# Latent attention: probabilities turned in 32x32 blocks by VectorE, values summed by eight tiles in four shared banks

## The reference

```python
q = (x @ W_q).reshape(B, S, 16, 128).transpose(0, 2, 1, 3)
latent = x @ W_kv_down                      # 64 wide
kv = (latent @ W_kv_up).reshape(B, S, 16, 128).transpose(0, 2, 1, 3)
scores = einsum('bhqd,bhkd->bhqk', q, kv) / sqrt(128)
probs = softmax(scores)
out = einsum('bhqk,bhkd->bhqd', probs, kv)
return out.transpose(0, 2, 1, 3).reshape(B, S, 2048) @ W_o
```

## Time and profile before

| | us |
|---|---|
| median of 3 runs | 1814.08 |
| lowest and highest | 1811.03 and 1816.03 |
| span of the profiled execution | 1840.4 |
| latent attention in it, first scores to last addition | 1195.4 to 1706.7 |

### The profile page before, as it was taken

One profiled execution on the slowest core, in us unless ns is written; L12 is line 12 of the kernel. 1 busy time (PEld: TensorE's weight loads), 2 busy tenths in 40 slices (PEclk: granted clock), 3 DMA queues, 4 the chain that ended last, 5 costly groups with the idle time before them and its releaser, 6 DMA issues. The chain is left out here.

```text
span 1840.4 us, 26235 instructions
## 1 busy us (share of the span) xinstructions
PE 1555.0 (84%) x7678; PEld 1023.0 (56%) x7678; DVE 1079.0 (59%) x2735; ACT 761.4 (41%) x1818; POOL 690.8 (38%) x677
## 2 busy tenths in 40 slices
PE   6889995548898978889993788689999999998798
PEld 3556654324455554555662566455666666665576
DVE  6842222376676547832224788477776766664788
ACT  5523332245555525533332111166655556553211
POOL 4553334454200003543335554055555545453000
PEclk9999997578999998999996888899999999999899
DMA  8319985122100005249972222000000000000000
GB/s 244 90 59 290 292 244 176 57 69 60 38 1 1 1 8 162 69 125 268 286 213 82 71 75 60 1 1 1 1 1 1 1 1 1 1 1 1 9 17 21
DMA packets 83395, 142.55 MB, mean 77 GB/s; under 512 B 15816, under 2 KB 43312, under 8 KB 83296
## 3 DMA queue, kind: packets, MB, share of 16 engines
q1 hardware_dynamic: 53600, 90.96, 17.0%
q0 software_dynamic: 15360, 37.77, 7.0%
q10 hardware_dynamic: 14336, 12.59, 2.5%
HBM read 122.39 MB, written 18.87 MB: 77 GB/s over the span
## 5 line engine op out<-in xcount | busy, mean ns | idle before, releaser
L2267 POOL TENSOR_TENSOR sb_m_prob<-sb_m_prob,sb_m_rinv 128x512 f32<-128x512 f32 x256 | 258.8, 1043 | 287.4 <-DVE sb_m_rinv L2316 287.4
L2223 ACT ACTIVATE sb_m_prob<-m_ps_s,sb_m_nmax 128x512 f32<-128x512 f32 x256 | 173.8, 683 | 204.1 <-DVE sb_m_nmax L2320 203.9
L1263 POOL DMA_INDIRECT sb_c_rows<-slot_rows,sb_slot x192 | 191.6, 998 | 130.7 <-DVEq L1284 57.9
L2320 DVE TENSOR_REDUCE sb_m_nmax<-m_ps_s 128x2 f32<-128x1024 f32 x128 | 156.4, 1222 | 127.8 <-PE m_ps_s L2118 127.8
L1097 POOL DMA_INDIRECT e_xn<-xn_rows,sb_table x128 | 118.0, 922 | 208.7 <-PE e_ps_x L1175 195.3
L1246 DVE TENSOR_TENSOR sb_e_h<-sb_e_sg,e_ps_gu 96x176 f32<-96x176 f32 x128 | 42.6, 333 | 255.2 <-ACT sb_e_sg L1222 208.7
L1184 PE MATMUL e_ps_gu<-e_wgu,sb_e_xT 128*96 128x352 f32 x512 | 177.2, 468 | 16.1 <-ACT sb_e_xT L1216 14.2
L2126 PE MATMUL m_ps_p<-sb_ident,sb_m_prob 128*128 128x128 f32 x1024 | 136.4, 273 | 15.8 <-ACT sb_m_pT L2231 11.3
L2126 PEld LDWEIGHTS m_ps_p<-sb_ident,sb_m_prob 128*128 128x128 f32 x1024 | 117.9, 141 | 41.2 <-POOL sb_m_prob L2267 13.8
L1201 PE MATMUL e_ps_y<-e_wdn,sb_e_hT 96*96 96x256 f32 x512 | 132.2, 382 | 0.0
L2117 PE MATMUL m_ps_s<-sb_m_latT_high,sb_m_qa 128*128 128x512 f32 x256 | 126.6, 495 | 1.1 <-ACT sb_m_prob L2223 1.1
(11 more groups left out here) (283 smaller groups left out, 3230.1 us busy)
## 6 DMA issues: line engine op xcount, KB each, us to landing
e_wgu<-wgu SPq DMA_DIRECT2D x128, 352.0 KB
e_wdn<-wdn SPq DMA_DIRECT2D x128, 192.0 KB
slot_rows<-sb_e_y ACTq DMA_DIRECT2D x128, 96.0 KB
xn_rows<-e_xn SPq DMA_DIRECT2D x16, 256.0 KB, 2.3
sb_c_rows<-slot_rows,sb_slot POOLq DMA_INDIRECT x192
sb_x<-x SPq DMA_DIRECT2D x4, 512.0 KB, 5.9
e_xn<-xn_rows,sb_table POOLq DMA_INDIRECT x128
sb_g_zm<-wqT SPq DMA_DIRECT2D x1, 2048.0 KB
```

Source lines behind the costliest of these rows:

```text
L1263: pool.indirect_dma_start(rows[u][j][:, :], None, k.slot_rows[:, :], bass.IndirectOffsetOnAxis(ap=k.slot[:, n, j:j + 1], axis=0))\
L2223: act.activation(prob[s % 4][:, hh, :], ps_s[s % 2][:, hh, :], ACT.Exp, bias=nmax[s % 2][:, hh:hh + 1], accum_out=rsum[s % 2][:, hh:hh + 1 ...
L2267: pool.tensor_tensor(part, part, rinv[s % 2][:, hh:hh + 1].to_broadcast([P, T]), ALU.mult)\
L2320: dve.tensor_reduce(nmax[s % 2][:, :], ps_s[s % 2][:, :, :], AX, ALU.max, negate=True).then_inc(nmax_ready, 1)
```

## The change

Only `latent_attention` changes; expert layers and linear attention stay as they are.

- The transposes on PE and both copies of them go. DVE turns each 32x32 block of `prob` in place of them, straight from SBUF to `pT`, one instruction a step (`probs_turned`), two steps behind. Blocks stay in their group of 32 partitions: partition group a then holds the probabilities of its own 32 queries of each tile, for 32 keys at a time, all 16 blocks of keys side by side.
- `values` becomes, for each of 16 blocks of 32 keys (kb), four partition groups (a) and two heads, a product of 32 rows x 64 columns x 128 columns of probabilities: 128 a pair. Group a sums into bank a of a `ps_v` that is now four banks. Half of a pair is made in each of two steps with s % 4 = 3 and 0.
- The latent must lie in each group of partitions with all keys: 16 DMAs a batch on SP's queue copy it from `lat` to `lat_rows`.
- The miscellany loses its own bank. It uses banks 0 and 1 of `ps_v` in turn, at steps with s % 4 = 1 and 2, and each of the two parts waits for the other: values for the eviction of the last two uses, the miscellany for the copy of the values.
- `oT_copy` goes from DVE to ACT, ahead of the exponentials of a step with s % 4 = 1.
- DVE's order becomes, for each s: row_max(s), probs_turned(s-2), inverse(s), and in steps with miscellany evictions(d) and preparations(d) of the same step. ACT's is oT_copy, exps(s), miscellany.
- The last two products with the output weights use the two banks too.

```diff
-    TLAG, VLAG = 3, 8
+    TLAG, VLAG = 2, 7
+    KB = T // TILE
...
-    bank_full, bank_free = k.sem("m_bank_full"), k.sem("m_bank_free")
+    bank_full, bank_free = k.sem("m_bank_full"), [k.sem(f"m_bank_free{v}") for v in range(2)]
     high_ready = k.sem("m_high_parts_ready")
     s_ready, nmax_ready, p_ready = k.sem("m_scores_ready"), k.sem("m_neg_max_ready"), k.sem("m_probs_ready")
     inv_ready, scaled = k.sem("m_inverse_ready"), k.sem("m_normalised")
-    pT_raw = [k.sem(f"m_pT_psum_ready{hh}") for hh in range(2)]
-    pT_ready = [k.sem(f"m_pT_ready{hh}") for hh in range(2)]
+    turned = k.sem("m_probs_turned")
+    lat_copied, lat_spread = k.sem("m_lat_copied"), k.sem("m_lat_spread")
...
-        lat = [sb(f"m_lat{u}", [P, TB, LAT]) for u in range(2)]
+        lat = sb("m_lat", [P, TB, LAT])
+        lat_rows = [sb(f"m_lat_rows{u}", [P, TB, TB, LAT]) for u in range(2)]
...
-        pT = [[sb(f"m_pT{u}_{hh}", [P, TB, T]) for hh in range(2)] for u in range(2)]
+        pT = [sb(f"m_pT{u}", [P, 2, TB, KB, TILE]) for u in range(2)]
         oT = [sb(f"m_oT{u}", [P, T]) for u in range(OSLOTS)]
         ps_s = [ctx.enter_context(nc.psum_tensor(f"m_ps_s{u}", [P, 2, T], F32)) for u in range(2)]
-        ps_p = [ps(f"m_ps_p{hh}", [P, TB, P]) for hh in range(2)]
-        ps_v = ps("m_ps_v", [P, T])
-        bank = ps("m_bank", [P, 512])
+        ps_v = ctx.enter_context(nc.psum_tensor("m_ps_v", [P, TB, T], F32))
...
+
+        def bank_of(key):
+
+            return ps_v[:, use_at[key] % 2, :]
+
+        def evicted(eng, key):
+
+            eng.wait_ge(bank_free[use_at[key] % 2], use_at[key] // 2 + 1)
+
+        def misc_at(s):
+
+            return s // TB * 2 + s % TB - 1 if s % TB in (1, 2) and s < NS else None
+
+        def last_use(s):
+
+            done = [misc_of(misc_at(x)) for x in range(s) if misc_at(x) is not None]
+            done = [use_at[key] for key in done if key is not None]
+            return max(done, default=5)
...
             def take(key):
-                if use_at[key]:
-                    pe.wait_ge(bank_free, use_at[key])
+                if use_at[key] >= 2:
+                    pe.wait_ge(bank_free[use_at[key] % 2], use_at[key] // 2)
+                return bank_of(key)
...
-            def probs_transposed(s, hh):
-                pe.wait_ge(scaled, 2 * s + hh + 1)
-                if s:
-                    pe.wait_ge(pT_ready[hh], s)
-                for t in range(TB):
-                    ins = pe.transpose(ps_p[hh][:, t, :], prob[s % 4][:, hh, t * P:(t + 1) * P], k.ident[:, :])
-                ins.then_inc(pT_raw[hh], 1)
-
-            def values(pair, t):
-                if t == 0:
-                    for hh in range(2):
-                        pe.wait_ge(pT_ready[hh], TB * (pair + 1))
-                    pe.wait_ge(bank_free, use_at[("lat", pair // PAIRS)] + 1)
+            def values(pair, half):
+                b, of = pair // PAIRS, pT[pair % 2]
+                if half == 0:
+                    pe.wait_ge(turned, TB * (pair + 1))
+                    pe.wait_ge(lat_spread, 256 * (b + 1))
                     if pair:
                         pe.wait_ge(o_copied, pair)
-                for hh in range(2):
-                    ins = pe.matmul(ps_v[rows_of(hh), :], lat[pair // PAIRS % 2][:, t, :], pT[pair % 2][hh][:, t, :],
-                                    start=(t == 0), stop=(t == TB - 1))
-                if t == TB - 1:
+                    last = last_use(TB * pair + VLAG)
+                    for n in (last - 1, last):
+                        evicted(pe, uses[n])
+                for kb in range(half * KB // 2, (half + 1) * KB // 2):
+                    for a in range(TB):
+                        rows = slice(a * TILE, (a + 1) * TILE)
+                        for hh in range(2):
+                            ins = pe.matmul(ps_v[rows_of(hh), a, 0:P], lat_rows[b % 2][rows, kb // TB, kb % TB, :],
+                                            of[rows, hh, :, kb, :], start=(kb == 0), stop=(kb == KB - 1))
+                if half == 1:
                     ins.then_inc(v_ready, 1)
...
-            for d in range(NR + VLAG // 2):
+            def miscellany(d):
...
-                for s in (2 * d, 2 * d + 1):
-                    if s < NS:
-                        scores(s)
-                    if 0 <= s - TLAG < NS:
-                        for hh in range(2):
-                            probs_transposed(s - TLAG, hh)
-                    if s == 2 * d and s >= VLAG:
-                        values((s - VLAG) // TB, (s - VLAG) % TB)
-                        values((s - VLAG) // TB, (s - VLAG) % TB + 1)
...
+                key = misc_of(d)
+                if key is None:
+                    return
+                if d >= 2:
+                    pe.wait_ge(o_copied, values_before(TB * (d // 2) + 1))
+                if key[0] == "lat":
                     latent_rows(b)
-                if e in Q_AT and b * PAIRS + Q_AT[e] < NP:
-                    queries(b * PAIRS + Q_AT[e])
-                if e in MIX_AT and b > 0:
+                elif key[0] == "q":
+                    queries(key[1])
+                elif key[0] == "mix":
                     half, t = MIX_AT[e]
-                    if t == 0:
-                        take(("mix", b - 1, half))
+                    bank = take(key) if t == 0 else bank_of(key)
                     ins = mixed(b - 1, 2 * half + t, bank[:, t * D:(t + 1) * D])
                     if t == 1:
                         ins.then_inc(bank_full, 1)
-                if e in TR_AT and b + 1 < B:
+                elif key[0] == "tr":
                     transposed(b + 1, TR_AT[e])
-                if e == LATT_AT and b + 1 < B:
...
+            def values_before(s):
+
+                return max(0, (s - VLAG - 2) // TB + 1)
+
+            for s in range(NS + VLAG - 2):
+                if s < NS:
+                    scores(s)
+                if s >= VLAG and (s - VLAG) % TB < 2:
+                    values((s - VLAG) // TB, (s - VLAG) % TB)
+                if misc_at(s) is not None:
+                    miscellany(misc_at(s))
+            pe.wait_ge(o_copied, NP)
+            bank = take(("mix", B - 1, 0))
             for t in range(2):
                 ins = mixed(B - 1, t, bank[:, t * D:(t + 1) * D])
             ins.then_inc(bank_full, 1)
+            bank = take(("mix", B - 1, 1))
             for t in range(2):
-                ins = mixed(B - 1, 2 + t, ps_s[0][:, 0, t * D:(t + 1) * D])
+                ins = mixed(B - 1, 2 + t, bank[:, t * D:(t + 1) * D])
...
-                    if s >= 4:
-                        act.wait_ge(pT_raw[hh], s - 3)
+                    if s >= 4 and hh == 0:
+                        act.wait_ge(turned, s - 3)
                     act.activation(prob[s % 4][:, hh, :], ps_s[s % 2][:, hh, :], ACT.Exp, bias=nmax[s % 2][:, hh:hh + 1],
                                    accum_out=rsum[s % 2][:, hh:hh + 1]).then_inc(p_ready, 1)
 
-            def pT_copy(s):
-                pair, t = s // TB, s % TB
-                act.wait_ge(pT_raw[1], s + 1)
-                if t == 0 and pair >= 2:
-                    act.wait_ge(v_ready, pair - 1)
-                act.activation(pT[pair % 2][1][:, :, t * P:(t + 1) * P], ps_p[1][:, :, :], ACT.Copy).then_inc(pT_ready[1], 1)
+            def oT_copy(pair):
+                act.wait_ge(v_ready, pair + 1)
+                act.activation(oT[pair % OSLOTS][:, :].rearrange("p (t a i) -> p a t i", a=TB, i=TILE),
+                               ps_v[:, :, 0:P].rearrange("p a (t i) -> p a t i", i=TILE), ACT.Copy).then_inc(o_copied, 1)
...
+            for s in range(NS + VLAG + 1):
+                if s >= VLAG + 2 and (s - VLAG - 2) % TB == 0:
+                    oT_copy((s - VLAG - 2) // TB)
+                if s < NS:
+                    exps(s)
+                if misc_at(s) is not None:
+                    miscellany(misc_at(s))
+
+        @block.sync
+        def _(sp):
+            for b in range(B):
+                sp.wait_ge(lat_copied, b + 1)
+                if b >= 2:
+                    sp.wait_ge(v_ready, (b - 1) * PAIRS)
+                for a in range(TB):
+                    for c in range(TB):
+                        sp.dma_start(lat_rows[b % 2][a * TILE:(a + 1) * TILE, :, c, :], lat[c * TILE:(c + 1) * TILE, :, :])\
+                          .then_inc(lat_spread, 16)
...
             def lat_copy(b):
-                full(("lat", b))
-                dve.tensor_copy(lat[b % 2][:, :, :], bank[:, 0:TB * LAT].rearrange("p (t l) -> p t l", l=LAT))\
-                   .then_inc(bank_free, 1)
+                key = ("lat", b)
+                full(key)
+                if b:
+                    dve.wait_ge(lat_spread, 256 * b)
+                dve.tensor_copy(lat[:, :, :], bank_of(key)[:, 0:TB * LAT].rearrange("p (t l) -> p t l", l=LAT))\
+                   .then_inc(bank_free[use_at[key] % 2], 1)
```

(43 more changed lines are left out.)

## The result

The changed kernel takes 1850.39 us (median of four runs, 1848.16 to 1853.39) against 1812.55 (four runs, 1807.21 to 1816.03): ratio 1.0213, 95% interval 1.0186 to 1.024. It is slower, as forecast, by 38 us rather than 18.5, at the upper edge of the forecast's own range (1817 to 1851).

What follows compares the result with a forecast made beforehand. TensorE bounds the kernel before, VectorE's order after; loop -2, clock +33, start -9.5 and end -3 sum to +18.5 us on 1814.1, rounded to 1833. Range 1790 to 1888, the forecast's own 1817 to 1851.

Steps and rivals of the forecast that it cites:

- Part 1: TensorE: transposes go, 0.88 us a step; half a pair of values takes 1.75 us plus 0.2 for the switch.
- Part 2: VectorE: a turn takes 1.22 us, covered by 1.5 us of waiting before the inverse; nothing on the path.
- Part 3: VectorE's order as new bound: 2.83 us a step, 2.32 more per query; loop 476 against 478.8, -2.
- behind values: Loop: first half of values waits for the previous step's evictions; 0.6 us about 14 times, 0.95 after three turned inputs: 12.
- Part 4: TensorE's clock falls in long idle gaps, slowing values and scores behind them: +33 us, bounds 0 and +50.
- Part 5: Ends of the stage: start -9.5 us, end -3 us; the spreading DMAs cost nothing.
- the clock holds: Rival: TensorE's gaps of 3 to 4 us leave the clock alone; 1798 us, chance 0.25.
- turns cost 2.09: Rival on VectorE: 3.3 us instead of 2.83 in some 70 steps; +30, 1863 us, chance 0.08.
- both cases of slow tiles: Rivals on TensorE: half a pair of values takes 2.6 us (1886, chance 0.09) or 3.5 us (1914, chance 0.08).

Runs made afterwards that it cites:

- e3: Changed kernel with VectorE turning each tile twice, the first time into a spare tile: 1876.88 us, ratio 1.0367.
- e5: Changed kernel with step 1's evictions behind the next row maximum and useless filler products on TensorE (fewer behind queries and turned inputs) together: 1787.47 us, ratio 0.9861.
- e2: Changed kernel with the evictions of steps with s % 4 = 1 made after the next step's row maximum: 1820.23 us, ratio 1.0043.
- e1: Changed kernel with useless filler products on TensorE where it would wait: 1830.53 us, ratio 1.0128.
- e7: Changed kernel with both halves of the values behind the scores of step 0 and every second block of 32 keys left out: 1803.36 us, ratio 0.9954.

## Why the prediction was right, and where its sum was short

The direction, the mechanism and the range held. The sum is 15 us short of what the stage shows (+18.5 against +33.5), and the measured median lies within 1 us of the upper end of the forecast's own range.

- *Part 1, right.* Half of the values: 1.95 predicted with the switch, 2.02 measured at the full clock, 128 records in 1.85 on the load side. PE was busy for 79% of the loop (about 75% was said of the stage). Eight tiles lose nothing to one another here. By the page "TensorE: Matmul & The Clock Gate" of the Trainium skill (Measured speedup vs the span model) a third of the gain would have gone and a half taken 2.6 us, an estimate from its figure for 16 tiles; the trace of these eight does not agree.
- *Part 2, right.* The turn took 1.236 (1.22 was taken), in the covering wait, as e3 bears out. By the page "VectorE: DVE Perf Modes" of the Trainium skill (The three transpose paths) my estimate was 2.5 us; with fp32 in 32x32 blocks the trace has half of it.
- *Part 3, right for the steps with evictions.* Predicted base 2.83 and query 5.15, measured 2.80 to 2.82 and 5.24. For columns 1 to 2 and 2 to 3 together the sum was 64 x 2.83 + 70 + 22 + 13 = 286; measured (4.36 + 4.62) x 32 = 287.
- *The term "behind values", mis-sized.* I gave it 12 us: 0.6 in 14 pairs and a little for three more. In fact the step behind the second half is 3.15 to 3.17 in 15 of the 32 pairs and longer in 11, since scores and values in PE's queue (0.95 + 2.02 and a start-up) are longer than 2.83, and the step behind the first is mostly 2.8 to 3.4 at the full clock, which e5 shows (mean 3.21). That is 0.38 x 32 from the first column of after and 0.38 x 31 from the fourth column of e5: 24 us. The first of these columns may hold some low clock too.
- *Part 4, right in kind; its size is bounded, not settled.* +33 was predicted. Bringing the clock from 0.91 to 0.99 took 29 us out of step 3 (e2 to e5); in the changed kernel itself filler took 21 out of step 3 and 14 out of the loop, with a third of the low clock still there (e1). That the size comes out near is in part luck, for the working was off: the gaps with two queries are mostly 4.9 to 5.4 us, not 4.4, and the low clock covers 106 us of the loop (0.90 over 523 us, a fifth of it), not 17 stretches of 3.4. PE is busy in 90 of these 106 us; at twice the clock that work would take some 45 less (an estimate), so part of the slow work was covered by the waits of PE for DVE behind it.
- *The pauses of PE for its instructions* had no term: 5.1 us, of which 1.7 lie in the loop and 3.4 behind the last row maximum.
- *Part 5, start exact* (-9.5 predicted, 28.06 to 18.61 measured), *end short by 1.4* (-3 predicted, 30.42 to 28.79), with the 3.4 us of pauses in it. The spreading transfers cost nothing, as said, although the waits of PE name them for 6.8 us, in two waits. This is a false releaser: in the timeline of the kernel after, the low parts end at 1439.95 and the values start at 1440.10, and the first values that need the latent being spread start at 1459.13.

```profile
1434.35 7.03 SPq L2298 DMA_DIRECT2D sb_m_lat_rows<-sb_m_lat  x11
...
1438.56 1.39 DVE L2339 TENSOR_TENSOR sb_m_qa<-m_ps_v,sb_m_qa 64x512 fp32r<-64x512 f32 x2 [0.91 <-ACT sb_m_qa L2245]
...
1440.10 1.29 PE L2158 MATMUL m_ps_v<-sb_m_pT,sb_m_lat_rows 32*64 32x128 f32 x52 [3.44 <-DMA sb_m_lat_rows<-sb_m_lat]
```

Added up again: 286 for steps 1 and 2; 63 x 2.83 = 178 for the other two, 24 behind values, 29 for the clock, 2 for the pauses: 519 of the 523.4 measured. This is no independent proof, since the 24 and the 29 are read off the columns that they explain. By it the 15 us are 12 of the values' term and 1.4 of the end, 2 of pauses, less the 4 by which the clock's term was high, and some 4 that have no term. The rest between 33.5 in the stage and 38 in the medians is in no trace; it is about the scatter of the runs.

The rivals: "the clock holds" fell with the window at 0.50; "turns cost 2.09" and both cases of slow tiles fell with the rows above. What stays open: the share of the clock in the changed kernel itself, since filler (e1) took only 14 us out of its loop while it lengthened other steps; 29 is from the pair e2 and e5. That the pauses are waits for instructions rests on the count of packets, on e7 and on the packets' times; no event of the profile names it.

## What to carry to other kernels

Work taken off the engine that sets the pace is worth only what the next engine's queue allows: here 0.88 us a step left PE, and the order of operations on DVE, where evictions stood between an inverse and the next row maximum, gave back all of it together with the lower clock. Before such a change, write out the queue of the engine that comes next and put what nobody waits for behind what everybody waits for; that one move was worth 25 us of the stage (30 in the medians). And TensorE with idle gaps was slower in its work as well here (granted clock 0.90, and 0.99 with the gaps filled): count the low clock for what is on the path behind each gap, and consider filling the gap. Last, compare a change of one stage by that stage: two executions of one program part that nobody touched differed by 24 us.

## What the runs showed of the hardware

- Eight tiles of 32 rows x 64 columns, writing four banks, 128 columns each: 128 records in 1.85 us, 14 ns apart, at the full clock; 3.36 at the low one. To the next product of another kind it was 2.02 and 3.65 us.
- A turn of 128x1024 fp32 in 32x32 blocks on DVE: 1.24 us, as long as a row maximum over the same elements (1.22).
- Small products use up instructions faster than they come: packets of 256 records, never closer than 3.2 us, against 2.0 us for 128 tile products and their loads. The program's packets went from 52 to 103; with two halves in a row 30.0 us of pauses stood before value products, each ending 1.2 to 1.6 us after the end of a packet.
- The low clock came with shorter gaps too: with gaps of PE of mostly 2.7 to 3.1 us before the values the granted clock was 0.91 over the loop (e2), with gaps mostly of 2.0 to 2.7 it was 0.83 (e7).
- More work on PE can make a kernel faster: with filler, 31 us of the stage (e2 to e5).
